# Sum by matmul, weights turned from int16, and hidden activations turned through DRAM in a gated d=2 block

## The chip, the cores and the metric

The kernel runs on one core of a Trainium2 chip. The time is the device time of one execution in microseconds (us), as the median of several runs. The profiled execution is a single one, so its sums are made against its own time.

## The reference

`x` and `ctx` are 8 batches of 256 channels by 512 positions, 4096 x 512 float32 in all: 16 tiles of 128 rows. Four sublayers run one after another, each with a tanh gate on a residual.

```python
x = x + tanh(g_xattn[0]) * L0_xattn(k=ln(ctx), ...)   # long convolution of k*v pairs, 32 heads of 8
x = x + tanh(g_ffn[0])   * L0_ffn(ln(x))              # int8-quantised 512 -> 2048 -> 512, exact GELU
x = x + tanh(g_xattn[1]) * L1_xattn(ctx, ln(x))       # softmax attention over 256 x 512, 8 batches
x = x + tanh(g_ffn[1])   * L1_ffn(ln(x))
# L1_ffn
rms = g * x * rsqrt(mean(x*x) + 1e-8)                 # also on the hidden rows, with g3
act = clip(round(rms * scale), -128, 127) / scale     # scale = 127 / max|row|
wq  = round(tanh(w / mean|w|)) * arctanh(mean|w|)     # ternary weights
h   = silu(act @ w1q.T) * (act @ w2q.T)               # 512 -> 2048
out = act_quant(rms(h)) @ w3q.T                       # 2048 -> 512
```

The exact operands of each sublayer do not matter here. What matters is that the second FFN quantises each row of its input and each row of its 2048 hidden values with that row's own maximum, and that its three weights are made ternary with the mean of their absolute values, a sum over a whole tensor.

## The kernel before

Each of the five engines has a program of its own, written out by hand; they meet only at counting semaphores. An engine works strictly in its program's order, so what is queued behind a waiting instruction waits too. Large buffers are cut by hand from one `arena` in SBUF (offsets in KB), and 16 KB more are `turn`. The stages run one after another with small overlaps.

First comes the convolution over 32 heads. A head's TensorE work is 20 matmuls (L997); ScalarE repeats columns (`repeat_q`, `repeat_c`), GpSimd makes pair products (`pairs`, L461) and adds halves (`add_halves`, L468), VectorE multiplies and adds (`head`, last instruction L1370). Two sets of four PSUM banks alternate by head. Beside it, ScalarE works on the ternary weights of the second FFN: heads 0 to 11 carry 48 sums of absolute values (`magnitudes`, L677). Then VectorE adds them to one column each of three (L1377), GpSimd adds those over all 128 partitions (`partition_all_reduce`, L485), VectorE makes three inverses (L1381 to L1385) and raises `binv_ready`. From then on ScalarE makes 48 tiles `tanh(w / mean)` as int16 (`ternary`, L685), in heads 15 to 29; SP stores each to `tern_d` in DRAM (L338) and loads the next raw tile (L329).

Next comes the first FFN, which ends with `mm2` (L1074) and the adding of its result to `x` in 16 tiles (`to_residual`, L1519). During it SP loads `ctx` again and all 48 ternary tiles from `tern_d` to `tern`.

Then the weights are turned: each of twelve groups of 128 x 2048 is widened from int16 to bf16 on VectorE or GpSimd (`tern_widen`, L1560, L540), transposed by TensorE in 16 pieces (`tern_T`, L962), and brought out of PSUM by ScalarE or VectorE (`tern_out`, L842, L1565). Seven groups stand before `project(0, 0)`, five between it and `scores(0, 0)`.

Attention runs over 8 batches. For one, TensorE does `project` of the next batch (L1128, L1133, L1141), `out_proj` of the batch before (L1199), transposes of the probabilities (L1152), the product with the values (L1181) and `scores` of the next (L1148). ScalarE does `proj_out` (two copies), `relu`, four copies of transposed probabilities, then the exponentials (`exps`, L857), which wait for VectorE's row maxima.

The second FFN takes 16 row tiles of 128. For tile t:
- x part, one tile ahead: `x_stats` (VectorE, mean and variance), `x_norm` (GpSimd, four small dependent steps ending in a power), `x_gain` (VectorE, L1642, two products of 512 columns), `x_max` and `x_scales` (VectorE, L1647 to L1657), `x_quant` (ScalarE, to int16), `x_widen` (VectorE, L1661, to bf16), `x_T` (TensorE, eight transposes), `x_out` (ScalarE, L897).
- `up`: four chunks of 512 columns, 8 matmuls each (L1219), with PSUM banks 3 and 5, or 4 and 6, in turn. A chunk waits for the `gate` two chunks before it. `silu` (ScalarE, L901) and `gate` (VectorE, L1730) empty the banks.
- hidden part: `h_gain` (GpSimd, L569, four products of 512), `h_squares` (ScalarE, L921), `h_rms` (GpSimd, three small steps), `h_max` (VectorE, L1736, four reduces), `h_scales`, `h_quant` (ScalarE, L907), `h_widen` (VectorE, L1755), `hidden_T` (TensorE, 16 transposes, L1227), `h_out` (ScalarE, L913), `down` (TensorE, 16 matmuls, L1237), `finish` (VectorE, L1760) and the store of the tile (SP, L399).

`hidden_T` and `down` of tile t-1 stand inside tile t.

## Time and profile before

| | us |
|---|---|
| median of three runs | 796.67 (796.19 to 798.14) |
| profiled execution, whole | 794.62 |
| its span, first to last instruction | 792.8 |
| TensorE busy | 677.3 (85%) |
| VectorE busy | 617.9 (78%) |
| ScalarE busy | 502.6 (63%) |
| GpSimd busy | 353.7 (45%) |
| TensorE's mean granted clock | 0.953 of full speed |

In the profile PE is TensorE, PEld its loading of stationary operands, DVE is VectorE, ACT is ScalarE, POOL is GpSimd, SP is SyncE, which here only starts DMAs. L12 is line 12 of the kernel before. A shape 128x512 is partitions by elements. The stretches in us from the start of the span are about: 0 to 55 loading and turning, 55 to 241 the 32 heads, 241 to 424 the first FFN, 424 to 449 the turning of weights, 449 to 572 attention, 572 to 793 the second FFN.

### The profile page before, as it was taken

Reading aid. Unit: us, or ns where it says so; the run is one execution under the profiler, and the core shown is the slowest. Engines: PE = TensorE matmul, PEld = TensorE weight load, DVE = VectorE, ACT = ScalarE, POOL = GpSimd, SP = SyncE. Lnnn points to the kernel's source line nnn. Section 1 sums busy time; section 2 is a strip of 40 time slices with the busy share of each in tenths; the row PEclk is TensorE's granted clock in tenths of the full one; section 3 lists DMA queues with packets and bytes.
Section 4 is the critical chain, followed back from the end, with each engine's and each line's share of the span. In section 5 each row is a group of like instructions: output and inputs, shape, how many; then the busy total and the mean of one; then the engine's idle time right before and its main releaser. Section 6 shows DMA issues by size and latency. Waiting matters only on the chain.

```text
span 792.8 us, 11907 instructions
## 1 busy us (share of the span) xinstructions
PE 677.3 (85%) x3476; PEld 404.4 (51%) x3476; DVE 617.9 (78%) x1108; ACT 502.6 (63%) x816; POOL 353.7 (45%) x436
## 2 busy tenths in 40 slices
PE   3659997699888479988797899999879999999996
PEld 2447775577666334443345565556434444444442
DVE  4876777377770948896989578888999999999983
ACT  3774673266544759896554644444568888888884
POOL 4536884788762500215832110011155555656552
PEclk9959999799998779999899999999999999999999
DMA  8953784288971401208582000000000000000000
GB/s 303 315 197 118 254 253 146 86 257 272 289 236 54 159 1 54 106 4 331 198 268 80 1 0 1 0 0 0 1 0 14 26 17 23 26 13 26 13 27 27
DMA packets 50047, 83.18 MB, mean 105 GB/s; under 512 B 6433, under 2 KB 19489, under 8 KB 48865
## 3 DMA queue, kind: packets, MB, share of 16 engines
q1 hardware_dynamic: 45664, 74.43, 28.1%
q10 hardware_dynamic: 4352, 8.39, 3.3%
q8 instruction: 14, 0.23, 0.1%
q14 instruction: 17, 0.13, 0.1%
HBM read 68.04 MB, written 14.76 MB: 104 GB/s over the span
## 4 chain that ended last, share of the span: by engine, by line
PE 33%; DVE 19%; ACT 15%; DMA 12%; issue 10%; POOL 5%; SPq 4%; ACTq 1%; DVEq 0%; POOLq 0%
PE ps L1039 5%; DMA tern_d<-late 4%; DMA late<-in_L_ffn_w 4%; PE ps L1074 4%; PE ps L997 4%; PE ps L1181 4%; PE ps L1148 3%; ACT arena L921 3%; DMA arena<-in_L_ffn_w 3%; DVE arena L1642 3%; ACT turn L814 2%; DVE q L1647 2%; PE ps L1128 2%; PE ps L1141 2%; DVE arena L1730 2%
## 5 line engine op out<-in xcount | busy, mean ns | idle before, releaser
L997 PE MATMUL ps<-arena 128*128 128x288 f32 x640 | 161.0, 414 | 18.8 <-POOL arena L462 12.3
L997 PEld LDWEIGHTS ps<-arena 128*128 128x128 f32 x640 | 123.1, 194 | 56.5 <-POOL arena L462 13.2
L1219 PE MATMUL ps<-arena 128*128 128x512 bf16 x512 | 116.2, 380 | 9.2 <-ACT arena L897 7.6
L569 POOL TENSOR_TENSOR arena<-arena 128x512 f32<-128x512 f32 x64 | 87.9, 1375 | 69.1 <-DVE arena L1730 68.9
L1219 PEld LDWEIGHTS ps<-arena 128*128 128x128 bf16 x512 | 47.4, 98 | 71.4 <-issue 14.2
L461 POOL TENSOR_TENSOR arena<-arena 128x1024 f32<-128x1024 f32 x32 | 60.9, 1902 | 26.7 <-ACT arena L656 17.9
L1360 DVE TENSOR_TENSOR turn<-ps,arena 128x768 f32<-128x768 f32 x32 | 30.6, 957 | 52.5 <-PE ps L997 49.0
L1074 PE MATMUL ps<-arena 128*128 128x512 bf16 x256 | 59.7, 398 | 10.9 <-DVE arena L1519 8.2
L1237 PE MATMUL ps<-arena 128*128 128x512 bf16 x256 | 61.7, 386 | 0.0
L1039 PE MATMUL ps<-arena 128*128 128x512 bf16 (+1 forms) x256 | 58.1, 385 | 1.8 <-ACT arena L768 1.7
L468 POOL TENSOR_TENSOR turn<-turn 128x512 f32<-128x512 f32 x32 | 40.8, 1276 | 24.3 <-DVE turn L1370 17.0
L901 ACT ACTIVATE arena<-ps,q 128x512 f32<-128x512 f32 x64 | 41.7, 674 | 14.9 <-PE ps L1219 14.9
L1074 PEld LDWEIGHTS ps<-arena 128*128 128x128 bf16 x256 | 25.7, 101 | 44.6 <-issue 17.3
L1730 DVE SCALAR_TENSOR_TENSOR arena<-ps,q,arena 128x512 f32<-128x512 f32 x64 | 47.5, 744 | 0.7 <-ACT arena L901 0.5
L768 ACT ACTIVATE arena<-ps,b,s 128x512 f32<-128x512 f32 x64 | 45.2, 794 | 3.7 <-PE ps L1039 2.7
L668 ACT ACTIVATE arena<-arena 128x512 f32<-128x512 f32 (+1 forms) x32 | 19.8, 621 | 41.9 <-DVE turn L1370 40.7
L1370 DVE TENSOR_TENSOR turn<-ps,turn 128x1024 f32<-128x1024 f32 x32 | 39.2, 1225 | 7.0 <-POOL arena L470 5.9
L1736 DVE TENSOR_REDUCE q<-arena 128x1 f32<-128x512 f32 x64 | 42.1, 677 | 1.7 <-POOL arena L569 1.6
L857 ACT ACTIVATE arena<-ps,nmx 128x512 f32<-128x512 f32 x32 | 21.8, 685 | 33.7 <-DVE nmx L1585 33.0
L907 ACT ACTIVATE arena<-arena,q 128x1024 int16<-128x1024 f32 x32 | 35.0, 1140 | 12.5 <-DVE q L1749 12.5
L1439 DVE TENSOR_REDUCE hmax<-arena 128x1 f32<-128x2048 f32 x15 | 34.0, 2277 | 9.8 <-ACT arena L768 9.8
L1039 PEld LDWEIGHTS ps<-arena 128*128 128x128 bf16 x256 | 24.8, 99 | 32.4 <-ACT arena L768 3.1
(206 smaller groups left out, 1451.0 us busy)
## 6 DMA issues: line engine op xcount, KB each, us to landing
arena<-in_L_ffn_w SPq DMA_DIRECT2D x72, 256.0 KB, 4.1
arena<-kpad_d ACTq DMA_DIRECT2D x16, 512.0 KB, 6.4
late<-in_L_ffn_w SPq DMA_DIRECT2D x24, 256.0 KB, 4.9
tern_d<-late SPq DMA_DIRECT2D x48, 128.0 KB, 4.2
arena<-in_x SPq DMA_DIRECT2D x4, 1024.0 KB, 12.2
arena<-in_ctx SPq DMA_DIRECT2D x4, 1024.0 KB, 13.4
arena<-in_L_ffn_w SPq DMA_DIRECT2D x4, 1024.0 KB, 11.7
x_d<-arena SPq DMA_DIRECT2D x4, 1024.0 KB, 4.2
```

Of the source, the lines that this page charges most:

```text
L461: pool.tensor_tensor(dst[:, :, 0:32].rearrange("p r (d i) -> p r d i", d=4), a, shifted, ALU.mult)
L468: po.done(pool.tensor_tensor(x[:, :, 0:16], x[:, :, 0:16], x[:, :, 16:32], ALU.add))
L569: pool.tensor_tensor(hg[:, s, sl], hh[:, s, sl], g3[:, sl], ALU.mult).then_inc(S["hg_done"], 1)
L768: act.activation(hid[:, q, f, :], ps[:, f % 4, :], ACT.Gelu, bias=b1[:, f:f + 1], scale=s1[:, f:f + 1]).then_inc(S["gelu_done"], 1)
L901: act.activation(sil[:, c, :], ps[:, 3 + c % 2, :], ACT.Silu, scale=q4[:, 11 + 2 * s:12 + 2 * s]).then_inc(S["sil_done"], 1)
L997: last = pe.matmul(ps[:, 4 * s + lo, 0:NB * PAIRS], toep[:, u, (lo - li) * P:(lo - li) * P + P], kv[:, s, li, :], start=(li == 0), stop=(l ...
L1039: last = pe.matmul(ps[:, f % 4, :], fw1T[:, k, f * P:(f + 1) * P], xqT[:, k, ds(L * r, L)], start=(k == 0), stop=(k == LB - 1))
L1074: return pe.matmul(ps[:, 2 * j + f // 8, :], hq[:, r % 2, f, j * P:(j + 1) * P], fw2T[:, f, :], start=(f % 8 == 0), stop=(f % 8 == 7))
L1219: last = pe.matmul(ps[:, 3 + 2 * j + c % 2, :], xq4T[:, s, 4 * j + k, :], w[:, k, c * L:(c + 1) * L], start=(k == 0), stop=(k == LB - 1))
L1237: last = pe.matmul(ps[:, 7, :], hqT[:, f, :], bw3T[:, f, :], start=(f == 0), stop=(f == FT - 1))
L1730: v.scalar_tensor_tensor(out=hh[:, s, c * L:(c + 1) * L], in0=ps[:, 5 + c % 2, :], scalar=q4[:, 12 + 2 * s:13 + 2 * s], in1=sil[:, c, :], ...
L1736: dv.done(v.tensor_reduce(q4[:, 32 + c:33 + c], hg[:, s, c * L:(c + 1) * L], AX, ALU.max, apply_absolute_value=True))
```

## The change

- The sums over partitions are made by one TensorE matmul with `mean_w` (every entry 1/128) into three spare columns of PSUM bank 0. TensorE's loop over heads is split after head 15: it waits for `bsum_ready` and the head products, does that matmul, waits for `binv_ready`, and goes on with head 16. VectorE waits for the matmul (`bsum_all`) between heads 14 and 15. The `ternary` work spreads over heads 16 to 29.
- `tern_d` is kept in the weights' own row order. SP turns it on the way in, with twelve DMA transposes of 512 x 512 int16 to the places of `bw1T`, `bw2T` and `bw3T`: four after `hqi_ready` 16, eight after `mm2_done`. The widening to bf16 is twelve in-place ScalarE copies (`values_widen`), two in each of attention blocks 1 to 6; before block 1 ScalarE waits for all twelve transfers. `tern_widen`, `tern_T` and `tern_out` are gone from all engines.
- In the second FFN, x is prepared two tiles ahead. The centring is a ScalarE instruction (`x_centre`, into `xc`), the product with both gains one GpSimd instruction of 128 x 1024 (`x_gain`). The quantised x goes out to DRAM and comes back turned, both from SP (`x_turned`).
- The hidden values go the same way (`h_turned`), except the last tile, which TensorE turns as before. `down(t - 2)` stands in tile t, its two halves between the chunks of `up`; `hqT` has two slots.
- `h_max` takes two reduces of 1024 columns in place of four of 512; the second stands in the next tile. `finish(t - 2)` moves behind `x_widen`.
- One ScalarE load of the Toeplitz tiles is issued before the second half of the `ternary` work of two heads, not after.

```diff
+            def turned(dst, w, n):
+                rows = tern_d[w].rearrange("(f k) -> f k", k=L if w < 2 else FF)
+                src = rows[n * L:(n + 1) * L, :] if w < 2 else rows[:, n * L:(n + 1) * L]
+                sp.dma_start_transpose(dst.bitcast(I16), src).then_inc(S["bw_in"], 16)
+
+            for n in range(4):
+                turned(bw1T[:, :, n * L:(n + 1) * L], 0, n)
             sp.wait_ge(S["mm2_done"], NT)
+            for n in range(4):
+                turned(bw2T[:, :, n * L:(n + 1) * L], 1, n)
+            for n in range(4):
+                turned(bw3T[:, 4 * n:4 * n + 4, :], 2, n)
...
+            def h_turned(t, s, past):
+                sp.wait_ge(S["hqb_ready"], 2 * t + 2)
+                if past is not None:
+                    sp.wait_ge(hT_in[s], 16 * past)
+                sp.dma_start(hq_d[s], hqb).then_inc(S["hq_stored"], 16)
+                sp.wait_ge(S["hq_stored"], 16 * t + 16)
+                if past is not None:
+                    sp.wait_ge(S["dn_done"], t - 1)
+                sp.dma_start_transpose(hqT[:, s], hq_d[s]).then_inc(hT_in[s], 16)
...
+            for t in range(1, NT):
+                h_turned(t - 1, (t - 1) % 2, (t - 1) // 2 or None)
+                if t >= 2:
+                    store(t - 2)
+                if t + 2 < NT:
+                    x_turned(t + 2, t % 2, t // 2 + 1)
...
-            pool.wait_ge(S["bsum_ready"], 1)
-            pool.partition_all_reduce(stot[:, :], scol[:, :], P, RED.add).then_inc(S["bsum_all"], 1)
...
+            def x_gain(t):
+                pool.wait_ge(S["xc_ready"], t + 1)
+                pool.tensor_tensor(xg[:, :, :], xc.unsqueeze(1).to_broadcast([P, 2, L]), g12[:, :, :],
+                                   ALU.mult).then_inc(S["xg_ready"], 1)
...
+            def ffn_body(t, s, nxt2):
+                if nxt2:
+                    x_norm(t + 2)
+                h_rms(t - 1)
+                if nxt2:
+                    x_gain(t + 2)
                 for c in range(4):
                     h_gain(t, s, c)
-                h_rms(t)
...
-                    for k in range(16 * (2 * i + u - 15) // 5, 16 * (2 * i + u - 14) // 5):
+                    for k in range(24 * (2 * i + u - 16) // 7, 24 * (2 * i + u - 15) // 7):
...
+            def values_widen(n):
+
+                w = bw_all[:, ds(n, 1), :].rearrange("p a k -> p (a k)")
+                act.activation(w.bitcast(BF16), w.bitcast(I16), ACT.Copy).then_inc(S["bw_ready"], 1)
...
+                if widen is not None:
+                    values_widen(widen)
                 if nxt:
                     exps(b + 1, 1 - p)
                 else:
                     relu(b - 1)
+                if widen is not None:
+                    values_widen(widen + 1)
...
+            act.wait_ge(S["bw_in"], 16 * 12)
             with act.Fori(0, NB // 2 - 1) as i:
                 for u in range(2):
-                    attn_body(2 * i + 1 + u, (1 + u) % 2, True, True)
+                    attn_body(2 * i + 1 + u, (1 + u) % 2, True, True, 4 * i + 2 * u)
...
+            pe.wait_ge(S["bsum_ready"], 1)
+            pe.wait_ge(S["prod_done"], HEADS // 2 + 1)
+            pe.matmul(ps[:, 0, NB * PAIRS:NB * PAIRS + 3], mean_w[:, :], scol[:, :], start=True, stop=True).then_inc(S["bsum_all"], 1)
+            pe.wait_ge(S["binv_ready"], 1)
+            with pe.Fori(0, HEADS // 8) as i:
+                four_heads(i + HEADS // 8)
...
+            def ffn_body(t, s, pair):
+
+                pe.wait_ge(xT_in[s], 16 * pair + 16)
+                up(t, s, (0, 1))
+                pe.wait_ge(hT_in[s], 16 * pair)
+                down(t - 2, s, 0, 8)
+                up(t, s, (2,))
+                down(t - 2, s, 8, FT)
                 up(t, s, (3,))
...
+            def ffn_body(t, s, nxt2, nxt3, prev, prev2):
+                u = s % 2
+                gate(t, s, 0)
                 if prev:
-                    h_scales(t - 1, 1 - s)
...
+                    h_max(t - 1, 1 - u, 1)
+                    h_scales(t - 1, 1 - u)
                 gate(t, s, 1)
                 if not prev:
                     latent_ln(NB - 1)
...
+                if nxt2:
+                    x_max(t + 2)
+                    x_scales(t + 2, (s + 2) % 4)
+                if prev:
+                    h_widen(t - 1)
                 gate(t, s, 2)
...
+                h_max(t, u, 0)
+                if nxt2:
+                    x_widen(t + 2)
+                if prev2:
+                    finish(t - 2, u)
                 gate(t, s, 3)
                 if not prev:
                     attn_end(NB - 1)
...
+                if nxt3:
+                    x_stats(t + 3)
```

## Rows read from the trace of the kernel before

**Rows 1.** Busy time of each engine by stretch: start:end, length, busy, clock, DMA

```profile
660.00:700.00 40.00, 37.66 (x223) 18.18 (x222) 38.84 (x84) 33.69 (x47) 22.82 (x34) 1.00 0.05 20
500.00:520.00 20.00, 20.00 (x85) 11.91 (x84) 17.25 (x44) 8.97 (x20) 2.19 (x5) 1.00 0.00 0
```

**Rows 2.** Chain of work that ended last, second FFN: start, duration, what

```profile
606.48 1.14 DVE q L1647
...
761.48 1.14 DVE q L1647
```

**Rows 3.** Instructions in order of time, heads 13 to 31: start, duration, engine, line

```profile
131.75 1.22 DVE L1370 TENSOR_TENSOR turn<-ps,turn 128x1024 f32<-128x1024 f32 x1
133.87 0.43 POOL L485 PARTITION_ALL_REDUCE stot<-scol  x1 [5.82 <-issue]
155.16 1.23 DVE L1370 TENSOR_TENSOR turn<-ps,turn 128x1024 f32<-128x1024 f32 x1
160.02 1.23 DVE L1370 TENSOR_TENSOR turn<-ps,turn 128x1024 f32<-128x1024 f32 x1
...
237.45 1.22 DVE L1370 TENSOR_TENSOR turn<-ps,turn 128x1024 f32<-128x1024 f32 x1
```

**Rows 4.** Who waited for whom, 60 to 250 us: total, times, longest

```profile
ACT late L685 <- DMA tern_d<-late: 26.0, 21, 3.7
```

**Rows 5.** Instructions in order of time, end of first FFN to first scores

```profile
426.37 0.69 DVE L1519 TENSOR_TENSOR arena<-turn,arena 128x512 f32<-128x512 f32 x1
...
429.20 3.65 ACT L842 ACTIVATE arena<-ps 128x2048 bf16<-128x2048 bf16 x2 [1.76 <-PE ps L962]
...
436.92 1.94 PE L1128 MATMUL ps<-arena,late 128*128 128x512 f32 x4
...
442.19 1.95 PE L962 MATMUL ps<-identb,turn 128*128 128x128 bf16 x32
...
449.54 2.81 PE L1148 MATMUL ps<-arena 128*128 128x512 f32 x6 [1.36 <-ACT arena L842]
```

**Rows 6.** DMA issues: what, queue, count, KB each, median us to landing

```profile
tern_d<-late SPq DMA_DIRECT2D x48, 128.0 KB, 4.2
...
arena<-tern_d SPq DMA_DIRECT2D x1, 4096.0 KB, 14.0
out_x<-arena SPq DMA_DIRECT2D x16, 256.0 KB, 2.0
...
b<-in_L_ffn_b SPq DMA_DIRECT2D x1, 8.0 KB, 11.6
```

**Rows 7.** Instructions in order of time, one attention block

```profile
499.36 0.69 ACT L857 ACTIVATE arena<-ps,nmx 128x512 f32<-128x512 f32 x1
...
503.87 1.88 PE L1199 MATMUL ps<-arena,late 128*128 128x512 f32 x4
```

**Rows 8.** Groups by line, 620 to 740 us: count, busy us, mean ns, idle before

```profile
L1642 DVE SCALAR_TENSOR_TENSOR arena<-arena,mv 128x512 f32<-128x512 f32 x18 | 21.8, 1252 | 0.0
```

**Rows 9.** Instructions in order of time, one steady tile of the second FFN

```profile
651.58 5.35 PE L1219 MATMUL ps<-arena 128*128 128x512 bf16 x24 [0.45 <-ACT arena L897]
...
652.99 0.19 POOL L558 TENSOR_TENSOR q<-mv,eps_ln 128x1 f32<-128x1 f32 x1
...
653.79 0.54 POOL L564 TENSOR_TENSOR q<-q,mhalf 128x1 f32<-128x1 f32 x1
...
656.79 0.75 DVE L1755 CAST arena<-arena 128x1024 bf16<-128x1024 int16 x2
...
658.13 1.20 DVE L1647 TENSOR_REDUCE q<-arena 128x2 f32<-128x1024 f32 x1
...
660.00 0.75 DVE L1730 SCALAR_TENSOR_TENSOR arena<-ps,q,arena 128x512 f32<-128x512 f32 x1
...
663.12 1.27 POOL L569 TENSOR_TENSOR arena<-arena 128x512 f32<-128x512 f32 x1 [1.02 <-DVE arena L1730]
```

**Rows 10.** The page's costliest groups: count, busy us, mean ns, idle before

```profile
L461 POOL TENSOR_TENSOR arena<-arena 128x1024 f32<-128x1024 f32 x32 | 60.9, 1902 | 26.7 <-ACT arena L656 17.9
```

More of the change, by code:

```diff
@@ L1664, in attn_body @@
                 if nxt and not nxt2:
-                    v.wait_ge(S["gs_in"], 48)
                     x_stats(0)
-                    x_gain(0)
-                    x_max(0)
+                if not nxt:
+                    x_max(1)
+                    x_scales(1, 1)
+                    x_stats(2)
                 if nxt2:
@@ L1677, in attn_body @@
                 if nxt and not nxt2:
+                    x_max(0)
                     x_scales(0, 0)
-                if not nxt:
                     x_stats(1)
-                    x_gain(1)
-                    x_max(1)
                 latent_stats(b)
@@ L1685, in attn_body @@
                     attn_end(b - 1)
-                    x_scales(1, 1)
+                    x_widen(1)
                 if nxt:
```

357 lines of the change are left out of this document (138 added, 219 removed).

## The prediction

> **What bounds the kernel now.** I read the busy table by stage first, then the chain of waits, then one tile of the second FFN in order of time. The stages have different limits. In the attention blocks TensorE is busy all the time and ScalarE under half [rows 1]: work moved to ScalarE there is nearly free, work taken off VectorE buys nothing. In the second FFN VectorE is busy 38.84 of 40 us and TensorE 37.66 [rows 1]. The chain of waits passes the same reduce (L1647) 13 times there, from 606.48 to 761.48 us [rows 2]: 12 periods, 155.0 / 12 = 12.92 us a tile. Two stretches in front of it are limited by no engine's throughput: a hole round the GpSimd all-reduce [rows 3], and the turning of twelve weight tiles between the first FFN and attention [rows 5].
>
> **1. Sum by matmul instead of the all-reduce.** VectorE's last instruction of a head (L1370) starts at 131.75 for head 13 and 155.16 for head 15 [rows 3]. Undisturbed heads are 4.86 us apart (155.16 to 160.02 [rows 3]). The hole is 23.41 - 2 x 4.86 = 13.7 us; the all-reduce itself shows 0.43 us, the rest is GpSimd waiting for nothing that the profile names, with the pair products of the next heads queued behind. All 13.7 go. A wait comes in: TensorE stops before head 16 until VectorE has made the inverses (three small operations) from a tiny matmul; the next head's 20 matmuls are queued behind it, and VectorE waits for that matmul ahead of head 15. No row has this chain. I take 1.0 us, five small steps of some 0.2, near the small steps of [rows 9]; at worst a whole head product that comes late, 2.8.
> Then something is given back. The 48 ternary values now ride on 14 heads (16 to 29), 3.43 each, before on 15 heads at 3.2. ScalarE already waited 26.0 us, 21 times, for their stores to DRAM [rows 4]. Heads 15 to 31 took 237.45 - 155.16 = 82.3 us [rows 3], 5.14 a head where 4.86 is free, so those stores partly limit this stretch. If a value has a fixed price (5.14 / 3.2 = 1.61 us), 14 heads take 14 x 3.43 x 1.61 = 77.3 and two free ones 9.7: 87.0, a loss of 4.7. If only the number of heads counts, none. I take 3.5, nearer to the fixed price because the waits are so many. Net 13.7 - 1.0 - 3.5 = **+9.2** (from 5 to 13).
>
> **2. Weights turned by DMA.** Today `scores(0, 0)` starts at 449.54. Without the twelve turns `project(0, 0)` needs only the last residual tile, finished at 426.37 + 0.69 = 427.1 [rows 5]. `project` takes TensorE from 436.92 to 442.19, 5.3 us [rows 5]. So scores can start at 432.4: **+17.1**. Cover: ScalarE now waits after block 0 for all twelve turned tiles, and every copy and exponential of the later blocks is queued behind that. The exponentials that end at 500.2 [rows 7] lie three blocks and their own 3 us behind the 449.54 of `scores(0, 0)`, so block 0 ends some 16 + 3 = 19 us after its scores, near 452; the last eight tiles (4 MB) may only start when the first FFN's matmuls are done, which I put 3.5 us ahead of the last residual tile, near 423.5. So a tile of 512 KB must take under 28.5 / 8 = 3.5 us. No row shows a turning transfer. From below: the plain load of the same weights, 4096 KB in 14.0 us [rows 6], 1.75 us a tile. From above: a load that goes element by element, 8 KB in 11.6 us [rows 6], which would be ruinous. I take 2.2, near the plain load, because the same long rows are read and only the writing side differs: hidden.
>
> **3. Widening inside attention.** Twelve ScalarE copies of 128x2048; two such took 3.65 us, 1.83 each [rows 5]. The first of a pair falls in the wait for the row maxima. The second sits ahead of `proj_out`: the exponentials end at 499.36 + 0.69 + 0.19 = 500.2 [rows 7], the widening at 502.0, two projection copies and the ReLU (about 2.0) at 504.1, while TensorE reaches `out_proj` at 503.87 [rows 7]. A delay of 0.3 in each of six blocks: **-1.8** (0 to -4).
>
> **4. The steady tile of the second FFN.** TensorE loses the turns and keeps 48 matmuls of 5.35 / 24 = 0.22 us [rows 9]: 10.4 to 10.7 us. VectorE loses two gain products (1.25 us each beside GpSimd [rows 8]) and swaps four reduces for two long ones: 12.92 - 2.4 - 0.2 = 10.3 us. ScalarE loses three copies for one. By busy time the tile would drop to about 10.6. But the product moved to GpSimd makes a ring with VectorE, and I walk it from the end of one tile's last `gate` to the next.
> On GpSimd, in program order: a handover of 0.1 and the last `h_gain`, 1.27 [rows 9]; `x_norm`, four dependent steps from 652.99 to 653.79 + 0.54 = 654.33, 1.34 [rows 9]; `h_rms`, three such steps (0.27, 0.27, 0.54), 1.1; then `x_gain`. Its price isn't in the trace. Lower end: the 128x1024 product of L461 with broadcast operands, 1.90 [rows 10]; upper end: two products of 1.27, 2.54. One operand of two is broadcast; I take 2.2. With a handover, 6.1 us.
> Then VectorE, in program order: `x_max` and `x_scales`, from 658.13 to 660.00, 1.87; `h_widen` 0.75; `gate` 2, 0.75; `h_max` over 1024 columns 1.20; `x_widen`, half of an `h_widen`, 0.4; `finish` and `gate` 3, like a gate, 1.5 [rows 9]. Neighbours overlap by about 0.07 each: 6.1 us. So the ring gives **12.2 us** (11.8 to 12.6), not 10.6: VectorE stands idle ahead of `x_max`. Twelve tiles (2 to 13) carry all this: 12 x 0.72 = **+8.6**.
>
> **5. Hidden tiles through DRAM.** `h_widen` ends 6.1 + 1.87 + 0.7 = 8.6 us into a tile. Its `down` stands in the next tile, and from the start of a `down` to the end of that tile's last gate lie 32 matmuls and a gate, 6.9 + 0.75 = 7.65. Over two tiles, 2P >= 8.6 + D + 7.65 with D the way out and back. At P = 12.2, D may be 8.1 us. A 256 KB store takes 2.0 us in a quiet stretch, a 128 KB one 4.2 in a busy one [rows 6]; I take 3 for 512 KB and 4.5 for the turning read with its start: D = 7.5, just hidden. SP works in order (hidden out, wait, back; result out; x out, wait, back), and stands still only for the two stores, some 5.5 of 12.2 us. x has two tiles' time, so its way is hidden.
> The Trainium skill ("DMA: Bandwidth & Descriptors", section "Latency and other measured facts") gives 261 GB/s for a turning DMA; by that, an estimate, 512 KB moves in 2.0 us, and steps 2 and 5 stay hidden. "Advanced Engine Details and Errata" of the Trainium skill, section "DGE: Hardware vs Software", rates the hardware generator, which this change uses, the worse of the two for transposes; that speaks for the third rival below. No row of this trace shows which holds.
>
> **6. The ends.** Tiles 0 and 1: +1 (the x products leave VectorE, but `x_max(1)` now stands ahead of the latent statistics and waits for GpSimd). Tile 14, free of x work, runs at TensorE's pace: +2.3. Tile 15 holds a `down` more: -2.5. The tail waits for hidden tile 14 by DMA, then does two `down` in place of one: -3. These are estimates from the prices above. Sum **-2.2** (from -8 to +3).
>
> **Sum.** 9.2 + 17.1 - 1.8 + 8.6 - 2.2 = 30.9. The profiled execution took 794.6 (span 792.8 and 1.8 around it); the median of the runs is 2.0 higher. 794.6 - 30.9 + 2.0 = **765.7 us**.
>
> **Rivals.**
> Main case, 0.53: as summed.
> R1, TensorE bounds the tile (0.12). If `x_gain` and its chain hide, P = 10.6: another 12 x 1.6 = 19 us, 747. For it: no engine's busy sum exceeds 10.7. Against it: the program order on GpSimd, `x_norm`, `h_rms` and `x_gain` in a row ahead of the first `h_gain`.
> R2, the way through DRAM becomes the ring (0.15). A lone transfer has a latency that a row of queued ones doesn't pay. With 6 us each way D = 12 and P = (8.6 + 12 + 7.65) / 2 = 14.1; 13 tiles lose 1.9 against the main case, 25 us: 791. For it: 4.2 us for small stores [rows 6]. Against it: 2.0 in the quiet stretch.
> R3, the other side: turning transfers are slow (0.20). At T us for 512 KB, ScalarE waits 8T - 28.5 after block 0, and in the FFN D = 3 + T. At T = 7 that is 27.5 us and P = 13.1 (12 us over the main case): 805, slower than before; the sign turns near T = 6.4. At T = 10: 51.5 and 31, 848. For it: no row shows such a transfer. Against it: the plain load at 1.75.
> That the change doesn't do what it says would be R3 at its extreme; the removed work is gone in every case.
>
> **Numbers.** A measurement of this kernel tells about 0.3%, 2.4 us, from no change. Faster: main, R1 and two thirds of R2, 0.75; within: 0.05; slower: 0.20. The range leaves out the slower end of R3 and the quickest of R1: 746 to 800.
>
> **What would show it.** In the changed trace: L1370's successor at an even 4.86 across heads 13 to 16, with one gap near 1 us; first scores near 423 (432.4 less 9.2); no wait of ScalarE on DMA after block 0; in the FFN VectorE's longest wait on GpSimd's product, tiles 12.2 apart. Wrong if TensorE waits on DMA ahead of `down`, if ScalarE stands before the first widening, or if SP's transfers queue one behind another.

## The result and the profile after

| | before | after |
|---|---|---|
| median | 796.43 us (793.24 to 798.14) | 787.09 us (786.02 to 787.43) |
| ratio, 95% interval | | 0.9885 (0.9852 to 0.9918) |
| profiled execution's span | 792.8 us | 785.2 us |

The change makes the kernel 1.1% faster: 9.3 us of the 30.9 forecast. The time lies inside the range, far above the forecast. (Ratios here and below leave out one slow execution, of the later `p1_only`: 1049.5 us at a mean granted clock of 0.65.) Five marks tell where the profiled pair's 7.6 us come from. (scores 0 and 7: first matmul of `scores` for batch 0 and 7. `up`: first matmul of tile 0. x_max: VectorE's reduce over x inside tiles 3 and 13.)

| stretch, us | before | after | gain |
|---|---|---|---|
| start to scores 0 | 449.54 | 426.47 | +23.1 |
| scores 0 to scores 7 | 108.56 | 108.49 | +0.1 |
| scores 7 to `up` | 14.41 | 20.26 | -5.9 |
| `up` to x_max of tile 3 | 46.83 | 49.83 | -3.0 |
| ten tiles, x_max of tile 3 to 13 | 129.28 | 133.70 | -4.4 |
| x_max of tile 13 to the end | 44.2 | 46.4 | -2.3 |

So all that was won was won before attention, and two thirds of it was given back after it. The last three rows have a shift in them: x_max stands 4.9 us ahead of its tile's last `gate` before, and 7.3 to 7.5 after, because other work was moved behind it. Counted by the end of the last `gate` of a tile, the second FFN is:

| stretch, us | before | after | gain |
|---|---|---|---|
| `up` to the last gate of tile 1 | 25.7 | 30.5 | -4.8 |
| tiles 2 to 13 | 155.3 | 160.6 | -5.3 |
| tiles 14, 15 and the end | 39.3 | 38.9 | +0.4 |

**Heads.** The changed trace in order of time round the new sum, then who waited for whom from 100 to 245 us:

```profile
132.09 1.22 DVE L1375 TENSOR_TENSOR turn<-ps,turn 128x1024 f32<-128x1024 f32 x1
139.04 1.23 DVE L1375 TENSOR_TENSOR turn<-ps,turn 128x1024 f32<-128x1024 f32 x1
...
144.49 1.22 DVE L1375 TENSOR_TENSOR turn<-ps,turn 128x1024 f32<-128x1024 f32 x1
...
150.27 1.23 DVE L1375 TENSOR_TENSOR turn<-ps,turn 128x1024 f32<-128x1024 f32 x1
...
129.78 11.53 PE L1020 MATMUL ps<-arena 128*128 128x288 f32 x40 [3.39 <-DVE turn L1375]
141.14 0.28 PE L1029 MATMUL ps<-scol,mean_w 128*128 128x3 f32 x2
142.48 1.72 PE L1020 MATMUL ps<-arena 128*128 128x288 f32 x6 [1.06 <-DVE inv_s L1390]
```

```profile
ACT late L708 <- DMA tern_d<-late: 27.2, 24, 2.9
```

Head 13 to head 15 takes 12.4 us where it took 23.4 [rows 3]: the hole is gone. TensorE's new wait for the inverses is 1.06, but the new place costs more than that wait. Two undisturbed heads take 9.7, so 2.7 are lost there, and head 16 comes 5.8 us behind head 15, 0.9 more than an undisturbed head. Ten of the sixteen traces with the new sum have 10.8 from head 13 to 15; in this one TensorE stood 3.39 us, and its next 40 matmuls took 11.53 us (9.94 in `p1_only`), with a granted clock of 0.75 from 130 to 136 us. Head 31's last instruction starts at 231.35 against 237.45, so 4.6 of the 11 us gained are lost again: 0.9 at head 16 and 3.7 behind it, where ScalarE waits for its value stores as long as it did [rows 4].

**Weights turned by DMA.** First scores of the changed trace, and its DMA issues from 400 to 440 us:

```profile
426.47 1.88 PE L1160 MATMUL ps<-arena 128*128 128x512 f32 x4
```

```profile
arena<-tern_d SPq DMA_TRANSPOSE x12, 5.2
```

They answer [rows 5]. Eight of the twelve are issued from 417.8 on, 2.6 us apart; the last lands at 441.0, ScalarE's first instruction of block 1 starts at 445.9, and ScalarE never waits for one.

**End of attention.** The same trace in order of time (engines apart):

```profile
530.77 3.51 DVE L1624 SCALAR_TENSOR_TENSOR arena<-turn,tg,arena 128x512 f32<-128x512 f32 x2
551.19 1.22 DVE L1638 TENSOR_REDUCE q<-arena 128x2 f32<-128x1024 f32 x1 [4.08 <-POOL arena L576]
...
531.07 2.67 POOL L576 TENSOR_TENSOR arena<-turn,arena 128x1024 f32<-128x1024 f32 x1
...
541.44 1.92 ACT L880 ACTIVATE arena<-arena  x1
...
541.62 2.79 PE L1164 MATMUL ps<-identf,arena 128*128 128x128 f32 x16 [2.94 <-ACT arena L870]
547.16 6.50 PE L1190 MATMUL ps<-arena 128*128 128x512 f32 x8 [2.76 <-DVE arena L1611]
...
557.83 2.57 DVE L1654 CAST turn<-turn 128x1024 bf16<-128x1024 int16 x1
...
557.66 2.46 POOL L576 TENSOR_TENSOR arena<-turn,arena 128x1024 f32<-128x1024 f32 x1 [1.57 <-ACT turn L919]
...
561.12 3.63 PE L1224 MATMUL ps<-arena 128*128 128x512 bf16 x16 [2.17 <-DVE arena L1709]
```

The busy row over the long matmuls (columns as in [rows 1]), and the same eight matmuls in the trace of before:

```profile
547.00:553.70 6.70, 6.54 (x9) 2.90 (x10) 2.47 (x7) 1.08 (x2) 3.92 (x5) 0.56 0.18 42
```

```profile
567.25 3.70 PE L1181 MATMUL ps<-arena 128*128 128x512 f32 x8 [1.12 <-DVE arena L1616]
```

Two residual additions (L1624) take 3.51 us while GpSimd makes its gain product; the same pair takes 1.42 elsewhere. The widening copy L880 stands ahead of the last probability copies. TensorE waits twice, and then does eight matmuls in 6.50 us where it took 3.70 before, at a granted clock of 0.56. Measured from scores 7, these eight start 3.05 us later than before (12.20 against 9.15) and last 2.8 longer, which is the 5.9 us. VectorE's wait of 4.08 us for x_max is not in it: it starts when the matmuls already run, and from them to `up` TensorE doesn't stop. In tile 0 the widening of x (L1654) takes 2.57 us beside GpSimd's product, 0.60 in a steady tile, and TensorE waits 2.17 us for the gates behind it.

**The steady tile**, GpSimd and VectorE of the changed trace from the end of one tile's last gate (679.68) to the next (692.97):

```profile
679.75 1.27 POOL L582 TENSOR_TENSOR arena<-arena 128x512 f32<-128x512 f32 x1 [1.68 <-DVE arena L1709]
680.99 0.19 POOL L563 TENSOR_TENSOR q<-mv,eps_ln 128x1 f32<-128x1 f32 x1
...
682.83 0.54 POOL L591 TENSOR_TENSOR q<-q,mhalf 128x1 f32<-128x1 f32 x1
683.34 2.35 POOL L576 TENSOR_TENSOR arena<-turn,arena 128x1024 f32<-128x1024 f32 x1
685.65 2.49 POOL L582 TENSOR_TENSOR arena<-arena 128x512 f32<-128x512 f32 x2
```

```profile
685.72 1.22 DVE L1638 TENSOR_REDUCE q<-arena 128x2 f32<-128x1024 f32 x1 [0.85 <-POOL arena L576]
686.98 1.20 DVE L1643 TENSOR_SCALAR q<-q 128x2 f32<-128x2 f32 x1
...
688.59 0.76 DVE L1737 CAST arena<-arena 128x1024 bf16<-128x1024 int16 x2
...
692.24 0.73 DVE L1709 SCALAR_TENSOR_TENSOR arena<-ps,up_scale,arena 128x512 f32<-128x512 f32 x1
```

The ring of step 4 (GpSimd and VectorE, each waiting for the other once a tile) is there: GpSimd's part lasts from 679.68 to 685.69, 6.0 us as forecast (6.1). VectorE's part lasts from 685.72 to 692.97, 7.25 us instead of 6.1. L1643, a multiply over two columns, takes 1.20 us; alone it takes 0.23 (at 552.52 in the same trace). It ends at 688.18, when GpSimd's second product ends (685.65 + 2.49 = 688.14). One busy row (busy us of TensorE, its loads, VectorE, ScalarE, GpSimd; granted clock, DMA share, GB/s) answers [rows 1], 640 to 680 us, with VectorE at 34.10 where it had 38.84: no engine is full, and the tile is longer all the same.

```profile
640.00:680.00 40.00, 32.97 (x149) 13.78 (x148) 34.10 (x70) 26.22 (x42) 27.88 (x37) 1.00 0.47 135
```

Its DMA issues, 600 to 740 us, with the median time to landing, answer what no row of before had:

```profile
hq_d<-arena SPq DMA_DIRECT2D x10, 512.0 KB, 2.6
...
arena<-hq_d SPq DMA_TRANSPOSE x11, 4.5
arena<-xq_d SPq DMA_TRANSPOSE x11, 3.2
```

### The profile page after: what moved, and what is told of

Read it like the earlier page. It is cut to its first block, busy times and chain, and to the rows that moved or that the text cites. A ratio compares the mean times of both kernels' runs of the same rounds, so it can differ in the third digit from the quotient of the medians.

```text
span 785.2 us, 10567 instructions
## 1 busy us (share of the span) xinstructions
PE 654.7 (83%) x2918; PEld 378.9 (48%) x2918; DVE 582.3 (74%) x1032; ACT 476.9 (61%) x789; POOL 371.1 (47%) x448
## 4 chain that ended last, share of the span: by engine, by line
PE 23%; issue 22%; DVE 18%; DMA 14%; POOL 11%; ACT 9%; SPq 1%; POOLq 1%; ACTq 0%; DVEq 0%
PE ps L1106 6%; PE ps L1071 5%; PE ps L1020 4%; DMA tern_d<-late 4%; DMA arena<-in_L_ffn_w 3%; POOL arena L576 3%; PE ps L1240 3%; DMA arena<-hq_d 2%; POOL arena L582 2%; PE ps L1224 2%; ACT arena L791 1%; DVE q L1638 1%; DMA hq_d<-arena 1%; DMA arena<-in_x 1%; DVE bn L1299 1%
## 5 line engine op out<-in xcount | busy, mean ns | idle before, releaser
L1020 PEld LDWEIGHTS ps<-arena 128*128 128x128 f32 x640 | 123.8, 195 | 50.6 <-POOL arena L483 9.9
L1224 PE MATMUL ps<-arena 128*128 128x512 bf16 x512 | 122.4, 390 | 15.9 <-DVE arena L1709 15.9
L582 POOL TENSOR_TENSOR arena<-arena 128x512 f32<-128x512 f32 x64 | 81.2, 1278 | 60.3 <-DVE arena L1709 60.1
L1224 PEld LDWEIGHTS ps<-arena 128*128 128x128 bf16 x512 | 50.1, 100 | 84.8 <-DVE arena L1709 24.1
L1240 PE MATMUL ps<-arena 128*128 128x512 bf16 x256 | 63.6, 395 | 24.5 <-DMA arena<-hq_d 23.9
L1106 PE MATMUL ps<-arena 128*128 128x512 bf16 x256 | 60.7, 402 | 10.1 <-DVE arena L1525 7.5
L1365 DVE TENSOR_TENSOR turn<-ps,arena 128x768 f32<-128x768 f32 x32 | 30.6, 957 | 50.2 <-PE ps L1020 49.1
L1709 DVE SCALAR_TENSOR_TENSOR arena<-ps,up_scale,arena 128x512 f32<-128x512 f32 x64 | 47.6, 745 | 12.6 <-ACT arena L924 10.5
L924 ACT ACTIVATE arena<-ps,up_scale 128x512 f32<-128x512 f32 x64 | 43.1, 673 | 18.1 <-PE ps L1224 17.8
L1240 PEld LDWEIGHTS ps<-arena 128*128 128x128 bf16 x256 | 24.4, 100 | 60.3 <-DMA arena<-hq_d 19.3
L1106 PEld LDWEIGHTS ps<-arena 128*128 128x128 bf16 x256 | 26.0, 102 | 44.5 <-issue 17.9
L1071 PEld LDWEIGHTS ps<-arena 128*128 128x128 bf16 x256 | 25.0, 100 | 32.6 <-ACT arena L791 3.1
L1716 DVE TENSOR_REDUCE q<-arena 128x1 f32<-128x1024 f32 x32 | 38.7, 1210 | 1.4 <-POOL arena L582 1.4
## 6 DMA issues: line engine op xcount, KB each, us to landing
arena<-in_x SPq DMA_DIRECT2D x4, 1024.0 KB, 12.1
arena<-in_ctx SPq DMA_DIRECT2D x4, 1024.0 KB, 13.3
```

Of the source, the lines that this page charges most:

```text
L582: pool.tensor_tensor(hg[:, s, sl], hh[:, s, sl], g3[:, sl], ALU.mult).then_inc(S["hg_done"], 1)
L924: act.activation(sil[:, c, :], ps[:, 3 + c % 2, :], ACT.Silu, scale=up_scale[:, s, 0:1]).then_inc(S["sil_done"], 1)
L1020: last = pe.matmul(ps[:, 4 * s + lo, 0:NB * PAIRS], toep[:, u, (lo - li) * P:(lo - li) * P + P], kv[:, s, li, :], start=(li == 0), stop=(l ...
L1071: last = pe.matmul(ps[:, f % 4, :], fw1T[:, k, f * P:(f + 1) * P], xqT[:, k, ds(L * r, L)], start=(k == 0), stop=(k == LB - 1))
L1106: return pe.matmul(ps[:, 2 * j + f // 8, :], hq[:, r % 2, f, j * P:(j + 1) * P], fw2T[:, f, :], start=(f % 8 == 0), stop=(f % 8 == 7))
L1224: last = pe.matmul(ps[:, 3 + 2 * j + c % 2, :], xq4T[:, s, 4 * j + k, :], w[:, k, c * L:(c + 1) * L], start=(k == 0), stop=(k == LB - 1))
```

## The experiments

Ratios are to the kernel before, on the same chip. All runs in one table, by the marks of the first table ("tile" is the mean of the ten; because of the shift of x_max, `up` to tile 3 and the rest compare only kernels with the same second FFN):

| kernel | scores 0 | 7 to `up` | `up` to tile 3 | tile | rest | median, ratio (interval) |
|---|---|---|---|---|---|---|
| before | 449.5 | 14.4 | 46.8 | 12.93 | 44.2 | |
| changed | 426.5 | 20.3 | 49.8 | 13.37 | 46.4 | 787.1, 0.9885 |
| old_ffn | 422.7 | 17.9 | 46.8 | 13.00 | 43.8 | 773.7, 0.9751 (0.9715 to 0.9787) |
| p1_only | 445.6 | 14.6 | 46.5 | 12.93 | 44.2 | 790.2, 0.9942 (0.9912 to 0.9973) |
| store_first | 425.2 | 20.4 | 49.1 | 13.33 | 46.9 | 786.0, 0.9871 (0.9834 to 0.9908) |
| early_widen | 425.5 | 15.9 | 51.8 | 13.29 | 47.5 | 785.5, 0.9878 (0.9833 to 0.9923) |
| old_ffn_early | 426.4 | 14.4 | 47.0 | 12.99 | 45.2 | 778.4, 0.9768 (0.9729 to 0.9808) |
| split | 426.3 | 20.5 | 49.6 | 13.16 | 47.4 | 785.5, 0.9878 (0.9834 to 0.9922) |
| swap | 431.5 | 20.6 | 46.6 | 13.08 | 48.1 | 786.1, 0.9884 (0.9840 to 0.9927) |
| split_swap | 424.6 | 20.7 | 47.1 | 12.78 | 47.4 | 780.9, 0.9842 (0.9806 to 0.9879) |
| one_column | 426.9 | 20.7 | 50.6 | 12.72 | 47.8 | 784.6, 0.9870 (0.9834 to 0.9905) |
| one_column_swap | 423.6 | 18.0 | 52.0 | 12.65 | 49.2 | 779.9, 0.9811 (0.9771 to 0.9851) |
| new_all | 425.7 | 17.7 | 52.5 | 12.48 | 47.4 | 784.7, 0.9870 (0.9833 to 0.9908) |
| half_gain | 426.4 | 18.0 | 45.8 | 12.21 | 46.9 | 770.7, 0.9682 (0.9649 to 0.9715) |
| gain_on_dve | 422.1 | 20.3 | 54.1 | 13.39 | 48.5 | 793.9, 0.9981 (0.9952 to 1.0009) |
| hybrid | 424.2 | 20.4 | 47.2 | 12.44 | 47.4 | 775.2, 0.9759 (0.9734 to 0.9784) |
| hybrid_early | 430.4 | 15.7 | 49.2 | 12.37 | 46.2 | 775.5, 0.9730 (0.9691 to 0.9768) |

From scores 0 to scores 7 every kernel took 108.5 us, those with early widening 110.2. Scores 0 varies by 9 us between kernels with the same front part (422.1 to 431.5), so small differences of medians mean little here, and the stretches mean more.

**1. Front parts against the new FFN.** `old_ffn` is the changed kernel with the second FFN of before, put back on all engines; TensorE's first waits there:

```diff
     pe.wait_ge(S["bw_ready"], 12)
-    pe.wait_ge(xT_in[0], 16)
+    pe.wait_ge(S["xT_out"], 1)
     up(0, 0, (0, 1))
```

> The changed kernel up to the end of attention, but with the second FFN of the kernel before: TensorE turns x and the hidden values, VectorE makes the gain products, `down` one tile later. Theory: the two front parts of the change brought 23.1 us (first scores at 426.5 against 449.5) and the new second FFN, with the end of attention, gave 14 of them away; so 796.4 - 23 = 773 us, FFN tiles of 12.9 us, and faster than the changed kernel's 787 by about 14. Rival: the part after attention became slower for a reason that lies in front of it (TensorE's granted clock after an earlier start, the in-place widening), not in the new FFN; then this kernel shows 12.9 us tiles lengthened too and ends near 785.

Measured 773.7 us. The theory stands: the new second FFN costs about 1.4% of the kernel, and undoing it alone gives a kernel faster than both. Of the 5.9 us lost at the end of attention, 3.5 are here too; its trace shows why:

```profile
536.17 1.90 ACT L823 ACTIVATE arena<-arena  x1
...
541.88 5.35 PE L1141 MATMUL ps<-arena 128*128 128x512 f32 x8 [1.12 <-DVE arena L1563]
```

The widening of block 6 delays the last copies by 1.9 us, TensorE's eight matmuls start 1.6 us later behind scores 7 than before, and they take 5.35 us in place of 3.70, at a granted clock of 0.69 (541.8 to 547.3).

**2. The sum alone.** `p1_only` is the kernel before with the first part of the change alone: the sum by matmul, the ternary work on heads 16 to 29, the Toeplitz load a step earlier.

> The kernel before with the first part of the change alone: the sums over partitions by a matmul, the ternary values in heads 16 to 29, the Toeplitz load one step earlier; everything behind is as before. Theory: the hole of 13.7 us goes, about 3 us come in at the new place and 4.6 us are given back by the value stores, so 6 us remain (the traces: head 31 at 231.4 against 237.5), ratio 0.992. Rival: the forecast's 9.2 us, ratio 0.988, if the trace's head stretch is an unlucky one; or nothing, if the first FFN absorbs an earlier start.

0.58%, 4.6 us (2.1 to 7.0), under the forecast's 9.2. The traces with the new sum take 85.5 to 89.8 us from head 15 to head 31 where before took 82.3. Then the stores' issue was moved ahead of the loads':

```diff
-                    if more:
-                        tern_load(...)
                     if second:
                         sp.dma_start(tdst[w]..., tint[:, c, :])
+                    if more:
+                        tern_load(...)
```

> The changed kernel with SyncE's order turned in the ternary stretch: for every value the store is issued ahead of the next load, not behind it. ScalarE waits 27 us there, 24 times, for the stores of the four slots (4.4 us to landing); the store's issue stands 0.4 to 0.5 us behind the load's. Theory: the round trip of a slot (value, issue, landing) limits this stretch, so 48 / 4 = 12 rounds shorten by 0.4 to 0.5 us each, 5 us of the 86.9 between heads 15 and 31. Rival: the transfers' own rate is the limit (254 GB/s, queues 75% busy), or the later load takes the store's place: no gain.

The stretch took 86.3 us, within those of the others. ScalarE now waits 27.2 us for the loads (21.4 and 5.8) in place of 27.2 for the stores: the rival. Which of rate and latency limits the transfers stays open.

**3. Widening earlier**, alone and with the old FFN:

```diff
+            values_widen(0)
+            values_widen(1)
-            with act.Fori(0, NB // 2 - 1) as i:
+            with act.Fori(0, NB // 2 - 2) as i:
...
+            attn_body(NB - 3, 1, True, True, 10)
+            attn_body(NB - 2, 0, True, True)
```

> The changed kernel with the widening copies one block earlier: two at the end of attention block 0, then two in each of blocks 1 to 5, none in block 6. From the scores of block 7 to the first `up` the kernel before took 14.4 us, the changed one 20.3, and the changed one with the old FFN 17.9. In the latter the second copy of block 6 (1.9 us) stands ahead of the quantised x and of the last copies of probabilities, and TensorE, having waited, does its next eight matmuls in 5.35 us in place of 3.70 at a lower granted clock. Theory: 1.9 + 1.6 = 3.5 us come back, 787 becomes 783.5, and that stretch 16.8 us. Rival: these 3.5 us have another cause, or block 0 now pays for it (ScalarE waits for the twelve transfers there): no gain.

> The front parts of the change with the second FFN of the kernel before (773.7 us so far), and the widening copies one block earlier (blocks 0 to 5). In the changed kernel that move gave 4.4 us back between the scores of block 7 and the first `up` and cost 1.75 between blocks 1 and 2. Theory: with the old FFN the stretch before the first `up` goes from 17.9 to 14.4 us as in the kernel before, block 1 pays 1.75: 1.7 us faster, 772, ratio to the kernel before 0.973. Rival: the two cancel, 773.7.

With the old FFN the stretch before `up` is back at exactly 14.4, and block 1 pays 1.7. So the copies cost nothing in blocks 1 to 5 and 3.5 us in block 6; the pair moved to the end of block 0 costs 1.7 us. The net 1.7 us can't be told by the medians (778.4 here, with scores 0 nearly 4 us later than in `old_ffn`). In the changed kernel 4.4 us come back before `up`, but 1.7 go in block 1 and 2.0 in tiles 0 to 3: 0.7 is left, which these runs can't tell from nothing (785.5 against 787.1; 783.5 was expected).

**4. The small multiply and GpSimd's order.** In `swap` the wait for `x_quant` moves along with `x_norm` and `x_gain`.

```diff
-   dv.done(v.tensor_scalar(q4[:, 7:9], q4[:, 5:7], q4[:, 4:5], CLIP_MIN, ...))
+   for j in range(2):
+       dv.done(v.tensor_scalar(q4[:, 7 + j:8 + j], q4[:, 5 + j:6 + j], q4[:, 4:5], CLIP_MIN, ...))
```

> The changed kernel with the first small multiply of `x_scales` (L1643, two columns, 1.2 us in the steady tile against 0.23 alone) written as two multiplies of one column. Theory: the two-column form waits until GpSimd's running product ends, one-column forms (h_scales, 0.21 us beside GpSimd) don't; so the two take 0.2 us each, the tile goes from 13.3 to about 12.5 us, and over 12 tiles 9 to 10 us go: near 777. Rival: VectorE waits for something else at that place (the power of `x_norm`, the reduce ahead of it, or GpSimd whatever the width); then the pair takes 1.2 to 1.4 us together and the time stays at 787.

```diff
-                if nxt2:
-                    x_norm(t + 2)
                 h_rms(t - 1)
                 if nxt2:
                     x_gain(t + 2)
+                    x_norm(t + 2)
```

> The changed kernel with GpSimd's order in a tile changed from x_norm, h_rms, x_gain to h_rms, x_gain, x_norm (the product doesn't need the power). Theory (the ring GpSimd, VectorE sets the tile): VectorE's wait of 0.85 us for the product ahead of `x_max` goes, and the power is made beside `x_max`; the small multiply still waits for a product of GpSimd, so the tile is 13.3 - 0.85 = about 12.5 us and the kernel ends near 787 - 10 = 777. Rival: the tile is set by the way of the hidden values through DRAM (TensorE waits 1.6 us a tile for it); then only that wait changes its place and the time stays within 2 us of 787.

> Both edits. Theory: they remove different terms of the same ring (0.85 and 1.0 us), so the tile is about 11.5 us, near where the way through DRAM sets the end (twice the tile >= 9.3 to the last widening + 7.2 for store and turning transfer + 7.65 = 24.1 for the tile as it is; with a ring shorter by 1.85 the first term is 7.5, so the tile can't be under 11.2), and the kernel ends near 787 - 12 x 1.8 = 765. Rival (DRAM sets the tile already): 787. If only one of the two counts: 777.

Each alone saved 0.4 us in an undisturbed tile (12.92 and 12.91 against 13.3), not 0.9; both together 0.5 (12.78). `split` and then `swap` show why, VectorE and GpSimd in order of time:

```profile
672.44 0.33 DVE L1644 TENSOR_SCALAR q<-q 128x1 f32<-128x1 f32 x2
672.81 0.17 DVE L1646 RECIPROCAL q<-q 128x2 f32<-128x2 f32 x1
672.89 0.73 DVE L1647 TENSOR_TENSOR up_scale<-q,ath 128x2 f32<-128x2 f32 x1
...
671.11 2.50 POOL L582 TENSOR_TENSOR arena<-arena 128x512 f32<-128x512 f32 x2
```

```profile
674.87 1.13 DVE L1643 TENSOR_SCALAR q<-q 128x2 f32<-128x2 f32 x1 [0.18 <-POOL q L569]
676.04 0.17 DVE L1645 RECIPROCAL q<-q 128x2 f32<-128x2 f32 x1
676.12 1.10 DVE L1646 TENSOR_TENSOR up_scale<-q,ath 128x2 f32<-128x2 f32 x1
...
674.71 2.49 POOL L582 TENSOR_TENSOR arena<-arena 128x512 f32<-128x512 f32 x2
```

In `split` the one-column pair is quick and the next multiply, of 0.14 us, waits until 673.6, the end of GpSimd's products. In `swap` L1643 waits until 676.0, the end of the first product (674.71 + 1.25), and L1646 until 677.2, the end of the second. Each wait is for the product that is running. So I wrote all three as one-column forms:

> The changed kernel with all two-column multiplies of `x_scales` as pairs of one-column ones (L1643, L1646, L1648; the two factors of ath as scalars). In the run that split L1643 alone the tile went from 13.29 to 12.92 us only, because the next two-column multiply took over the wait (0.73 us against 0.14) and ended again with GpSimd's second product. Theory: a two-column form waits for GpSimd's running product, a one-column form doesn't; `x_scales` takes about 1.0 us in place of 1.6, the ring GpSimd, VectorE gives 6.0 + 6.6 = 12.6 us a tile, the kernel ends near 787 - 8 = 779. Rival: what waits is whatever instruction comes there, and the wait moves on once more (to the last multiply or to `h_widen`); then 12.9 us and 783 as in that run.

> The same, and GpSimd's order h_rms, x_gain, x_norm. With that order VectorE no longer waits for the product, and the tile is VectorE's own sum: 12.91 us as measured, of which 1.9 us are two waits of small multiplies for GpSimd's two products (1.13 and 1.10 us against 0.23 and 0.14). Theory: without these waits the tile is 11.1 to 11.5 us and the kernel ends near 787 - 12 x 1.9 = 764. Rival 1: the waits move on to another instruction: 12.8 us, 781 as with L1643 alone split. Rival 2: the hidden values' way through DRAM becomes the ring; TensorE now has 1.9 us of slack behind it, so it would set in just under 11 us a tile.

With `one_column` alone the tile is 12.7 us, near the 12.6 expected. With the order changed too the wait moved on, to the widening (`one_column_swap`; such a pair takes 0.75 undisturbed):

```profile
666.87 1.89 DVE L1741 CAST arena<-arena 128x1024 bf16<-128x1024 int16 x2
...
665.78 2.69 POOL L582 TENSOR_TENSOR arena<-arena 128x512 f32<-128x512 f32 x2
```

Rival 1 holds: what waits isn't one badly shaped instruction, it moves on to the next of the same kinds that VectorE runs beside a product. The Trainium skill ("SBUF — State Buffer", section "SBUF: two separate sides") states the rule behind it: VectorE, in a two-port mode or with two SBUF inputs (these only against a GpSimd instruction that reads SBUF, as all of the products here do), and GpSimd share one pair of ports as an exclusive lock, and the one that starts first keeps it for its whole instruction. The rows agree. One-column multiplies, reciprocals, reduces and gates that read PSUM run beside GpSimd undelayed; two-column multiplies, products of two SBUF operands and the widening wait. By that rule L1624's 3.51 us and the 2.57 of L1654 in tile 0 are the same thing. No run here looks at the ports themselves.

`new_all` adds the early widening and moves `x_max`, `x_scales` and `x_stats` in the last two blocks behind the row maxima and `attn_end`.

> The changed kernel with all mends: one-column multiplies, GpSimd's order h_rms, x_gain, x_norm, early widening, and in the last two attention blocks `x_max`, `x_scales` and `x_stats` behind the row maxima and behind `attn_end`. Theory: 779.9 us with the first two; the early widening brings 2.6; the order at the end of attention takes VectorE's wait for GpSimd (4.1 us at 547) off the path to the first `up`, 2 to 4 us: 774 to 776. Rival: the wait only moves to tile 0 and 1, which need the same products: 777.

The steady tile is that of `one_column_swap`, 12.5 us (one short period of 11.7 brings the mean to 12.48). From scores 7 to tile 3 it takes 17.7 + 52.5 = 70.2 us where `one_column_swap` takes 70.0, and 784.7 is no better. The order gives nothing back before `up`: `early_widen`, with the old order, has 15.9 there and this kernel 17.7, because the normalising of the last probabilities now stands behind `x_max` and `x_scales`, and TensorE waits 4.39 us for it in place of 2.94. The 4.08 us at 547 that the theory wanted to remove were never on the path to `up`.

The totals expected in this section were all missed, by 6 to 16 us (777, 777, 765, 779, 764 and 775 against 785.5, 786.1, 780.9, 784.6, 779.9 and 784.7). The tile got shorter by less than was expected, and the tiles before and behind the ten gave part of it back: with `one_column_swap` they take 5.0 us more than in the changed kernel.

**5. The product's length.** `half_gain` leaves out the second gain's product, and `x_max` and `x_quant` read the first for both, so it doesn't compute the reference; it prices the product.

```diff
-  pool.tensor_tensor(xg[:, :, :], xc.unsqueeze(1).to_broadcast([P, 2, L]), g12[:, :, :], ALU.mult)
+  pool.tensor_tensor(xg[:, 0, :], xc, g12[:, 0, :], ALU.mult)
```

> The changed kernel with GpSimd's `x_gain` over 512 columns in place of 1024: the second gain's product isn't made, the first serves for both (the result is another one). It costs GpSimd about 1.2 us in place of 2.36. Theory (ring of GpSimd and VectorE, with the small multiply's wait for GpSimd in it): VectorE's wait ahead of `x_max` (0.85) goes and the multiply's wait shrinks by 0.3, so a tile takes 12.1 to 12.2 us in place of 13.3: near 774. Rival (VectorE's own sum or the hidden values' way through DRAM sets the tile): 12.9 us or more, 782 to 787.

The tile is 12.21 us, as expected; the total is better than expected (770.7) because the end of attention and tiles 0 to 3 gain 6.3 us too (63.8 in place of 70.1). With the same transfers as in the changed kernel, this also clears the way through DRAM up to here. Then the product back on VectorE, or shared:

```diff
+            def first_gain(t):
+                v.wait_ge(S["xc_ready"], t + 1)
+                dv.done(v.tensor_tensor(xg[:, 0, :], xc, g12[:, 0, :], ALU.mult))
...
-                pool.tensor_tensor(xg[:, :, :], ...)
+                pool.tensor_tensor(xg[:, 1, :], xc, g12[:, 1, :], ALU.mult)
```

> The changed kernel (with the one-column multiplies) without the product on GpSimd: VectorE makes both gain products as in the kernel before, two tiles ahead, between h_scales and the second gate; ScalarE's centring falls away. Everything through DRAM stays. Theory (GpSimd's 2.36 us on the ring and VectorE's waits for GpSimd's products are what costs): VectorE's own sum is 11.1 us a tile without waits, 1.4 us come for the products, and they and the widening fall in gaps of GpSimd, so 12.5 us a tile, no loss at the end of attention against the kernel before but the widening (17.9 us from scores 7 to the first `up`), near 773. Rival (the way through DRAM or preparing two tiles ahead costs): 13 us or more a tile, 783 or more.

> The changed kernel (with the one-column multiplies) with the gain product shared: GpSimd makes the second gain's half (1.2 us), VectorE the first's (0.7 us, right behind the first gate, while GpSimd does small steps). The result is the same as the changed kernel's. Theory: GpSimd's part of the ring is 6.0 - 1.15 = 4.9 us and VectorE's 6.6 to 6.9, and VectorE's products and widenings fall in gaps of GpSimd: 12.0 us a tile (the run with half a product had 12.2), near 771, a ratio of 0.968. Rival: VectorE waits for GpSimd at the new product or at `h_widen`: 12.6 us, 779.

> The same with the widening copies one block earlier. In the pair with the old FFN that move gave back 3.45 us before the first `up` and cost 1.75 in block 1. Theory: 1.7 us faster than the shared product alone. Rival: with the x parts of the new FFN in the last block only 2.6 of it comes back, as in the changed kernel: 1 us, which three rounds can't tell.

`gain_on_dve` went the rival's way in time (13.25 us in an undisturbed tile, and 4.3 more than the changed kernel before the mark in tile 3), though not by its reason. VectorE in order of time, one tile:

```profile
669.45 0.21 DVE L1731 TENSOR_SCALAR q<-q 128x1 f32<-128x1 f32 x1 [0.39 <-POOL q L589]
...
670.03 1.74 DVE L1634 SCALAR_TENSOR_TENSOR arena<-arena,mv 128x512 f32<-128x512 f32 x2
...
680.25 0.75 DVE L1716 SCALAR_TENSOR_TENSOR arena<-ps,up_scale,arena 128x512 f32<-128x512 f32 x1 [0.55 <-ACT arena L922]
```

VectorE idles 0.39 and 0.55 us of a 13.25 us tile, and no `gate` there waits for matmuls. The tile is VectorE's own chain: its instructions take 12.3 us, near my 12.5 (which had not counted the 0.3 that the product loses to GpSimd), and the two waits, 0.9 together, were left out. So the product costs too much on either engine. Shared, it costs half on each, and an undisturbed tile is 12.1 us (x_max at 662.19, 674.29, 686.28, 698.45), near the 12.0 expected; the total is 775.2 against 771. `hybrid_early` gets 4.7 us back before `up`, pays 1.7 in block 1 and 2.0 in tiles 0 to 3, and its median is the same. In `hybrid` two of the ten take 13.4 and 14.2. The first ran at a full clock, though TensorE had waited 2.63 us in it. TensorE in the second, by time and then by stretch (columns as above, the clock third from the end):

```profile
697.30 3.28 PE L1239 MATMUL ps<-arena 128*128 128x512 bf16 x8 [1.99 <-DMA arena<-hq_d]
700.37 2.24 PE L1223 MATMUL ps<-arena 128*128 128x512 bf16 x8
```

```profile
686.00:697.00 11.00, 9.31 (x44) 4.02 (x41) 10.13 (x23) 8.36 (x13) 7.58 (x13) 1.00 0.57 165
697.00:700.50 3.50, 3.20 (x9) 1.22 (x10) 3.22 (x13) 2.19 (x2) 3.42 (x3) 0.59 0.24 58
```

After 1.99 us of waiting for the turned hidden values the granted clock is 0.59 over 3.5 us, mostly the lower of its two levels (1.2 GHz, where 1.00 is 2.4 GHz); eight matmuls take 3.28 us in place of 1.89, and the gate behind them waits 1.27 us for TensorE. The changed kernel has one such tile (630 us, clock 0.67, 14.06 us long). Waits that cost nothing by themselves cost this at times. `hybrid` and `old_ffn` beat both kernels, the changed one by 1.3 to 1.4% (by their ratios to before; they were not run beside it).

## Why the prediction was right or wrong

Direction and range were right, 21.4 us of the amount were wrong. In the profiled pair 23.3 of the 30.9 us are missing: 13.9 in step 4, 3.1 in step 1, 1.7 in step 3, and 4.6 in step 6, where errors of both signs meet. By steps, in that pair (forecast gain, measured):

- **Step 1 (+9.2, 6.1).** The hole was right, and the give-back nearly (3.7 behind head 16, 3.5 taken). The price of the new place was not: the 1.0 taken covers TensorE's wait for the inverses, 1.06, but the place costs 3.6, of which 0.9 show at head 16 and 1.6 come with slow matmuls that ten of the other traces don't have. `p1_only` has 4.6 us (2.1 to 7.0) as a median.
- **Step 2 (+17.1, 17.0).** Right, its cover too: eight transfers issued in 21 us, 2.6 each, under the limit of 3.5; the 2.2 taken and the 2.0 estimated were both low.
- **Step 3 (-1.8, about -3.5).** The mechanism, `out_proj` late by 0.3 in each of six blocks, doesn't exist: seven blocks took 108.49 us against 108.56. The price is in one place I didn't walk, the copy in block 6 ahead of the last block's own copies, with a slower TensorE behind. `old_ffn_early` takes it away whole, for 1.7 us in block 1.
- **Step 4 (12 x 0.72 = +8.6, -5.3).** The ring was the right mechanism, and the price that the trace lacked, GpSimd's product, was close: 2.35 for 2.2. The failed step is VectorE's term "`x_max` and `x_scales`, from 658.13 to 660.00, 1.87" [rows 9]: 2.87 in the new place. That term makes 1.0 of the 1.15 us by which VectorE's part is longer than forecast, and the tile 13.3 where 12.2 was due. I copied a duration from a moment in which GpSimd's product was ending as the first multiply started to one in which two of its products run back to back. The trace of before, at the place that I copied:

```profile
658.28 1.27 POOL L569 TENSOR_TENSOR arena<-arena 128x512 f32<-128x512 f32 x1 [1.96 <-DVE arena L1730]
659.36 0.23 DVE L1652 TENSOR_SCALAR q<-q 128x2 f32<-128x2 f32 x1
```

The page before had the sign: two gain products at 1252 ns each [rows 8], which take 0.74 where no product runs. The measured parts add up, 6.0 + 7.25 = 13.3, and shortening the product by 1.15 gave 12.2.

- **Step 5 (hidden, hidden).** D, the way of the hidden values out and back, is 2.6 + 4.5 = 7.1 us against 7.5 taken and 8.1 allowed. TensorE does wait for it, 1.6 us a tile, and nobody waits for TensorE; only the clock makes some of it count. Down to a tile of 12.1 us it isn't the ring.
- **Step 6 (-2.2; tiles 0 and 1 -4.8, tiles 14, 15 and tail +0.4, and 2.4 lost at the end of attention).** All three parts were off. Tiles 14, 15 and the tail were put at +2.3, -2.5 and -3, and are +1.6, -0.5 and -0.7. Tiles 0 and 1 were put at +1; tile 0 alone loses 3.9, with the widening of x held up by GpSimd's product. The end of attention wasn't in the sum beyond step 3: the residual additions beside the product lose 2.1, the row maxima stand behind them, and TensorE starts its eight matmuls 1.5 us later than in `old_ffn` and does them 1.15 slower. `x_max(1)` ahead of the latent statistics, which I had named and priced within +1, does wait 4.08 us for GpSimd, but costs nothing before `up`.

**The rivals.** R1 (TensorE bounds the tile): no; the ring, 13.3, lies above TensorE's 10.6. R2 (the way through DRAM is the ring): no, D is 7.1. R3 (slow turning transfers): no, 4.5 us for 512 KB, below the turning point of 6.4; in the queue 2.6. The rival that came true was none of mine: GpSimd's new work slows VectorE's instructions beside it.

## What to carry to other kernels

When work moves from VectorE to GpSimd, reprice every VectorE instruction that will run beside it, not only the one moved: a duration holds for the moment it was read in. Look for rows at two prices (0.74 and 1.25 for the same gain product in the trace of before) before counting an engine's sum, and compare stretches by marks behind which the same work is left. And undo each part by itself: here one part of the change hid that the other two were worth 2.5%.
